# A graph layer with sorted edges: three searches for the node offsets instead of two, x split on GpSimd, eight edge blocks ahead of round 0

## The reference

```python
h = x @ W_node.T + b_node
e = edge_attr @ W_edge.T + b_edge
msg = (h[src] + e) @ W_msg.T + b_msg
s = segment_sum(msg, dst); deg = segment_sum(1, dst)
out = layernorm(x + s / maximum(deg, 1)[:, None])
```

## Time and profile before

| | before |
|---|---|
| median of 3 runs (lowest to highest) | 811.5 us (810.43 to 813.04) |
| profiled execution, time | 810.29 us |
| profiled execution, span | 808.4 us |
| busy: PE, weight load, DVE, ACT, POOL | 726.8, 643.4, 636.3, 461.0, 49.9 us |
| mean granted TensorE clock | 0.939 |
| moved by DMA | 121.08 MB |

### The profile page before, as it was taken

One profiled execution on the slowest core, in us unless ns is written; L12 is line 12 of the kernel. 1 busy time (PEld: TensorE's weight loads), 2 busy tenths in 40 slices (PEclk: granted clock), 3 DMA queues, 4 the chain that ended last, 5 costly groups with the idle time before them and its releaser, 6 DMA issues.

```text
span 808.4 us, 24794 instructions
## 1 busy us (share of the span) xinstructions
PE 726.8 (90%) x10555; PEld 643.4 (80%) x10555; DVE 636.3 (79%) x1128; ACT 461.0 (57%) x938; POOL 49.9 (6%) x42
## 2 busy tenths in 40 slices
PE   3454636999999999999999999999999999999995
PEld 2333435988898899889889888988888988898895
DVE  6564998798789878888888888878887887788732
ACT  4343632666566566565656665666666656565641
POOL 2002100000000000000000000000000000000000
PEclk9655657999999999999999999999999999999998
DMA  7987431544535444544553465346334544454300
GB/s 223 248 266 232 154 106 54 167 135 155 163 122 177 161 151 138 174 130 137 186 174 119 127 208 168 97 140 221 122 124 156 173 156 128 165 169 134 99 15 15
DMA packets 71529, 121.08 MB, mean 150 GB/s; under 512 B 4486, under 2 KB 17502, under 8 KB 71315
## 3 DMA queue, kind: packets, MB, share of 16 engines
q1 hardware_dynamic: 68462, 115.72, 44.8%
q0 software_dynamic: 2336, 2.83, 1.3%
q10 hardware_dynamic: 618, 0.90, 0.5%
HBM read 116.18 MB, written 3.23 MB: 148 GB/s over the span
## 4 chain that ended last, share of the span: by engine, by line
PE 85%; DVE 7%; DMA 4%; issue 2%; ACT 1%; ACTq 0%; DVEq 0%; POOLq 0%
PE x_ps L581 49%; PE count_ps L565 18%; PE win_ps L513 12%; PE win_ps L520 3%; DMA edges<-in_edge_attr_dram 2%; PE misc_ps L597 1%; PE misc_ps L598 1%; DVE key_hot L709 1%; DVE x_rest L879 1%; DMA win_src<-in_src_dram,clipped_int 1%; DVE row_hot L803 1%; DMA region<-in_dst_dram 1%; DVE row_hot L709 1%; DVE x_rest L873 1%; DMA starts_dram<-edge_total 1%
## 5 line engine op out<-in xcount | busy, mean ns | idle before, releaser
L1167 ACT CAST region<-count_ps 128x490 bf16<-128x490 f32 x625 | 350.2, 574 | 174.1 <-PE count_ps L565 168.0
L581 PE MATMUL x_ps<-region,x_rest 128*128 128x250 bf16 x2450 | 449.3, 270 | 0.0
L581 PE MATMUL x_ps<-region,x_hi 128*128 128x250 bf16 x1225 | 332.6, 271 | 0.0
L709 DVE TENSOR_TENSOR row_hot<-iota_bf,row 125x3200 bf16<-125x3200 bf16 x125 | 227.8, 1822 | 94.6 <-PE count_ps L565 64.3
L565 PE MATMUL count_ps<-key_hot,row_hot 125*128 125x98 bf16 x3125 | 244.2, 209 | 28.3 <-DVE key_hot L709 28.2
L565 PEld LDWEIGHTS count_ps<-key_hot,row_hot 125*128 125x128 bf16 x3125 | 199.8, 99 | 57.0 <-DVE key_hot L709 29.9
L581 PEld LDWEIGHTS x_ps<-region,x_rest 128*128 128x128 bf16 x2450 | 229.6, 98 | 17.4
L709 DVE TENSOR_TENSOR key_hot<-iota_bf,key 125x2500 bf16<-125x2500 bf16 x125 | 181.7, 1454 | 0.0
L513 PE MATMUL win_ps<-edges,onehot 128*32 128x128 f32 x3232 | 118.7, 292 | 11.2 <-DMA edges<-in_edge_attr_dram 9.4
L581 PEld LDWEIGHTS x_ps<-region,x_hi 128*128 128x128 bf16 x1225 | 118.9, 97 | 8.0
L513 PEld LDWEIGHTS win_ps<-edges,onehot 128*32 128x32 f32 x3232 | 89.0, 116 | 32.6 <-issue 21.8
(11 more groups left out here) (166 smaller groups left out, 318.6 us busy)
## 6 DMA issues: line engine op xcount, KB each, us to landing
edges<-in_edge_attr_dram SPq DMA_DIRECT2D x101, 1024.0 KB, 5.6
resid<-in_x_dram SPq DMA_DIRECT2D x25, 125.0 KB
out_dram<-y SPq DMA_DIRECT2D x25, 125.0 KB
region<-in_dst_dram ACTq DMA_DIRECT2D x1, 768.0 KB
win_src<-in_src_dram,clipped_int POOLq DMA_INDIRECT x25, 6.6
region<-in_L_gnn_W_node_dram SPq DMA_DIRECT2D x1, 64.0 KB
region<-in_L_gnn_W_edge_dram SPq DMA_DIRECT2D x1, 64.0 KB
region<-in_L_gnn_W_msg_dram SPq DMA_DIRECT2D x1, 64.0 KB
```

Source lines behind the costliest of these rows:

```text
L581: mm = pe.matmul(x_ps[m % 2][:, 0:NB], rows, counts[m % 2][:, b, :], start=(n == 0), stop=(n == PARTS - 1))
L709: ins = dve.tensor_tensor(hot[0:WE, g % 2, :, :].rearrange("p w (a b) -> p w a b", b=4), iota_bf[0:WE, 0:width].rearrange("p (c a b) -> p ...
L1167: act.copy(counts[m % 2][:, :, f * FILL * 2:(f + 1) * FILL * 2], count_ps[fill % COUNT_BANKS][:, 0:FILL * KEYS].rearrange("p (n b) -> p b ...
```

## The change

- `LEAD` is 8 instead of 11. The 93 other blocks lie in the 125 slots of the rounds, where 90 did; in rounds 0 and 1 there are four each, as before, in rounds 2 to 24 there are 85 instead of 82.
- Three searches: job 0 serves rounds 0 and 1 alone (5 columns, a window of 375 entries, columns of at most 332), job 1 rounds 2 to 17 (31 columns, 1375 entries, 13 columns on DVE and 18 on ACT), job 2 rounds 18 to 24 (14 columns, 750 entries, columns of at most 326). Job 0 is counted at block 1, job 1 in segments 0 to 2, job 2 in segments 4 and 5. All three windows are asked for in the lead; DVE prepares the block counts of job 1 (one instruction) ahead of the placing offsets of the first block.
- `x` (3.2 MB) is loaded behind block 3 instead of block 9, the weights behind block 6 instead of block 2; the weights are folded in segments 0 to 2 instead of blocks 4 to 6, and waited for at the first `apply_counts`.
- `split_rest` and `split_low` run on POOL, ahead of `load_window` of rounds 2 to 24. Their input, `copy_hi`, runs on ACT at blocks 5 to 7 and in segments 0 and 1. The first `apply_counts` still waits for all of them.
- `make_slots` of job 1 is in segment 5, of job 2 in segment 8, with the degrees, which wait for the latter; `make_keys(2)` moves from the second to the third segment of round 1.
- The checks move to segments 12 to 18; `check_order` reads the turned offsets (128x404, 4 parts) instead of the untouched ones (101x2048).
- Buffers: the windows lie elsewhere in `region`, `before_hot`, the junk outputs and `rows_words` have room of their own, and the turned slots and degrees go to `misc_ps` (`free_misc` is what PE waits for ahead of it).

```diff
-LEAD = 11
+LEAD = 8
-    JOB_K = (36, 14)
-    JOB_L = (1650, 825)
-    JOB_DVE = (18, 7)
+    JOB_K = (5, 31, 14)
+    JOB_L = (375, 1375, 750)
+    JOB_DVE = (3, 13, 4)
+    JOB_ROWS = (2, B_ROUNDS - 2, G0)
+    JOB_ROUND = (0, 2, B_ROUNDS)
+    SLOTS_B, SLOTS_A, DEGREES = 5, 8, 8
...
@@ sync
                 load_edges(t)
-                if t == 2:
+                if t == 3:
+                    load_x()
+                if t == 6:
                     load_small()
-                if t == 9:
-                    load_x()
...
@@ gpsimd
-            load_job(0)
-            load_job(1)
-            for m in range(ROUNDS):
+            def split_rest(i):
+                words = x_rest[:, i * 7:(i + 1) * 7, :].rearrange("p b d -> p (b d)")
+                pool.wait_ge(x_hi_ready, i + 1)
+                pool.tensor_tensor(words, words, x_hi[:, i * 7:(i + 1) * 7, :].rearrange("p b d -> p (b d)"), ALU.subtract).then_inc(x_rest_ready, 1)
+
+            def split_low(i):
+                words = x_rest[:, i * 7:(i + 1) * 7, :].rearrange("p b d -> p (b d)")
+                pool.wait_ge(x_rest_ready, i + 1)
+                lower, upper = halves(words)
+                pool.tensor_tensor(lower, words, upper, ALU.subtract).then_inc(x_ready, 1)
+
+            for k in range(JOBS):
+                load_job(k)
+            for m in range(2):
+                load_window(m)
+            for i in range(7):
+                split_rest(i)
+            for i in range(7):
+                split_low(i)
+            for m in range(2, ROUNDS):
                 load_window(m)
...
@@ tensor
+            def free_misc():
+                if ends[0] > 0:
+                    pe.wait_ge(msg_added, 2 * ends[0])
+                if turns[0] > 0:
+                    pe.wait_ge(keys_spread, turns[0])
+                if misc_slots[0] > 0:
+                    pe.wait_ge(src_index_ready, misc_slots[0])
+                if misc_degrees[0] > 0:
+                    pe.wait_ge(deg_copied, 1)
...
-                    if t == 8:
+                    if t == 4:
                         turn_slots(0)
                     place_windows(t)
-                    if t == 5:
-                        make_weights()
-                    if t == 9:
+                    if t == 6:
                         turn_keys(0)
...
+                    if f == 4 and g == 0:
+                        turn_weights()
+                    if f == 4 and g == 1:
+                        make_weights()
-                    if f == 3 and g == 2:
+                    if f == 1 and g == SLOTS_B:
+                        turn_slots(1)
+                    if f == 1 and g == SLOTS_A:
+                        turn_slots(2)
+                    if f == 3 and g == DEGREES:
                         turn_degrees()
-                        turn_slots(1)
...
@@ vector
             begin_job(0)
+            block_counts(1)
...
+                    if g < 3:
+                        count_nodes(1, [0, 4, 9][g], [4, 9, 13][g])
                     if g == 0:
+                        dve.wait_ge(wm_turned, 1)
+                        link(dve.tensor_copy(wm_t, x_ps[0][:, 0:D]))
...
+                    if g == 2:
+                        end_job(1)
+                        copy_weights()
+                        dve.sem_inc(early_done, 1)
+                    if g == 4:
+                        count_nodes(2, 0, JOB_DVE[2])
+                    if g == 5:
+                        make_slots(1)
+                        end_job(2)
+                    if g == SLOTS_A:
+                        make_slots(2)
                         make_degrees()
-                        check_order()
-                    if g == 1:
-                        check_sorted()
-                    if g == 2:
-                        make_slots(1)
-                        check_slots()
-                        copy_degrees()
-                        for i in range(7):
-                            split_rest(i)
-                    if g == 3:
-                        for i in range(7):
-                            split_low(i)
-                        dve.sem_inc(early_done, 1)
+                        copy_degrees()
...
@@ scalar
+                    if t == 1:
+                        sign_counts(0, JOB_DVE[0], JOB_K[0])
+                    if t == 2:
                         send_starts(0)
+                    if t == 3:
                         fetch_starts(0)
+                    if t >= 5:
+                        copy_hi(t - 5)
+                    if t == 6:
                         spread_keys(0)
...
-                if g in (1, 2):
-                    for i in range(4 * (g - 1), min(4 * g, 7)):
+                if g < 2:
+                    for i in range(3 + 2 * g, 5 + 2 * g):
                         copy_hi(i)
+                if g < 3:
+                    sign_counts(1, [13, 19, 25][g], [19, 25, 31][g])
+                if g == 3:
+                    send_starts(1)
+                if g == 4:
+                    fetch_starts(1)
+                    sign_counts(2, JOB_DVE[2], 9)
+                if g == 5:
+                    sign_counts(2, 9, JOB_K[2])
```

More of the change, by code:

```diff
@@ L146, in gnn_layer @@
         pos = sb("pos", [P, NS])
[L148 to L151, removed]
+        before_hot = [words.rearrange("p (j n) -> p j n", j=TILES) for words in before_words]
+        act_junk = [sb(f"act_junk{k}", [PB, 580], BF16) for k in range(2)]
+        dve_junk = [sb(f"dve_junk{k}", [PB, 580], BF16) for k in range(2)]
         is_last = sb("is_last", [P, 1])
@@ L166, in gnn_layer @@
[L166 to L171, removed]
+        lent = sb("lent", [P, 4 * P])
+        before_node = [lent[:, k * P:k * P + PB] for k in range(JOBS)]
@@ new lines, in gnn_layer @@
+        pos_nat = lent[:, 3 * P:4 * P].rearrange("p (q w) -> p q w", q=Q)
+        job_node = [sb(f"job_node{k}", [PB, JOB_K[k]]) for k in range(JOBS)]
+        job_half = [sb(f"job_half{k}", [PB, JOB_K[k]]) for k in range(JOBS)]
+        job_low = [sb(f"job_low{k}", [PB, JOB_K[k]]) for k in range(JOBS)]
+        job_high = [sb(f"job_high{k}", [PB, JOB_K[k]]) for k in range(JOBS)]
+        job_off = [sb(f"job_off{k}", [PB, JOB_K[k]]) for k in range(JOBS)]
+        job_cnt = [sb(f"job_cnt{k}", [PB, JOB_K[k]]) for k in range(JOBS)]
@@ L178, in gnn_layer @@
+        limit = [sb(f"limit{k}", [JOB_ROWS[k], 1]) for k in range(JOBS)]
         first_slot = sb("first_slot", [PB, 3, ROUNDS])
@@ L353, in halves, with window @@
             return both[:, :, 0], both[:, :, 1]
+        def window(k, i):
+            return max(0, LOWEST[k][0] * i + LOWEST[k][1]), HIGHEST[k][0] * i + HIGHEST[k][1]
         block = ctx.enter_context(nc.Block())
@@ L458, in load_window @@
             def load_window(m):
-                pool.wait_ge(src_index_ready, 1 if m < B_ROUNDS else 2)
+                pool.wait_ge(src_index_ready, 1 + sum(1 for r in JOB_ROUND[1:] if m >= r))
                 if m >= 3:
@@ new lines, in check_order @@
+            def check_order(i):
+                part = rel_col[:, 4 * i:4 * (i + 1), :]
+                junk = win_a.bitcast(BF16)[:, 0:4 * NS].rearrange("p (t c) -> p t c", t=4)
+                link(dve.tensor_scalar(junk, part, 0.0, None, ALU.is_ge))
+                link(dve.scalar_tensor_tensor(junk, part, float(W), junk, ALU.is_lt, ALU.mult, accum_out=inside[:, i:i + 1]))
+                if i == 3:
+                    link(dve.tensor_reduce(viol[:, 0:1], inside[:, :], AX.X, ALU.add))
```

292 lines of the change are left out of this document (145 added, 147 removed).

## The result

The changed kernel took 808.9 us (median of 10 runs, 805.22 to 810.03) beside 812.08 us for the kernel before (10 runs, 810.39 to 816.43): ratio 0.9946 (95% interval 0.9923 to 0.9969). The forecast was 796.8, range 788 to 807. The sign was right; of the forecast gain of some 15 us, 3 came. The profiled execution took 809.33 us, span 807.5, against the span of 808.4 before. The two profiled executions thus differ by 1 us only, the medians by 3.2: the one of before lay 1.8 us under its median of these ten runs, the one of after 0.4 above.

The account below looks back on a forecast made before the run. Data bounds the lead, DVE round 0, PE the rest. Lead -19.4, round 0 -8.6, POOL's pieces +4.9, round 1 +4, blocks +4.4 sum to -14.7: 795.6 profiled, 796.8 us median, range 788 to 807.

Parts of the forecast that it names:

- The sign: Whole kernel: faster, at a chance of 0.95; slower 0.04, within 0.3% 0.01.
- The lead: Stretch before round 0, bound by data: first hots at 61.8 instead of 81.2 us, -19.4 us.
- 12 us at 246 GB/s (2.95 MB), the other 3.41 MB at 295 GB/s: In the lead from 20.9 us: 6.36 MB moved at these rates, so block 4 has landed at 44.5 us.
- the rival with x holding up the slots: In the lead: x ahead of block 4 delays the slots more, at 6 us more 802.5 us; chance 0.1.
- The rate of 246: In the lead: the DMA rate in GB/s while windows of `dst` are fetched beside the edges, taken for 12 us.
- From block 4 to the first hots: End of the lead: slots turned, neighbour lists fetched and keys made between block 4's landing and first hots, 17.3 us.
- Round 0: First hots to first product with x: 38.4 us instead of 47.0 (-8.6), with POOL and DVE taking turns 43.3 (+4.9).
- Round 1: After the first product with x: new waits in segments 5 and 8 cost +4 us, from 0 to 7.
- The waits: Round 1, PE: for job 1's slots in segment 5, for job 2's slots and the degrees in segment 8, about 2 us.
- ACT's last columns: Round 1: DVE's `end_job(2)` waits for ACT's last five columns, about 1.5 us.
- Blocks: Rounds 2 to 24: three more blocks where PE is the limit, sums and placing, +4.4 us.
- A piece: One subtraction of x's split on POOL: 1.74 us, between bounds of 0.87 and 2.6.

Follow-up runs that it names:

- e5: The changed kernel with the windows of jobs 1 and 2 asked for only when x is in: 808.64 us (one run).
- e1: The changed kernel with x loaded behind block 7 and copied on ACT in segments 1 and 2 of round 0: 804.83 us.
- b1: The kernel before with only the 14 pieces of x's split moved to POOL, behind the windows of rounds 0 to 2: 817.09 us, ratio 1.0045.
- e6: The changed kernel with the edits of e1 and e4 together: 801.6 us, ratio 0.9873 to the kernel before.
- e9: e6 with each subtraction on POOL cut in two, 28 instead of 14: 802.33 us, ratio 0.9876 to the kernel before.
- e7: e1 with copies of x in segments 0 and 1 and job 2's window asked for behind the lists of rounds 0 and 1: 806.11 us.
- e2: The changed kernel without the 14 subtractions that split x; PE multiplies the upper part three times instead: 798.7 us (one run).
- e3: The changed kernel with the 14 subtractions back on DVE, in segments 2 and 3 of round 0: 815.33 us, ratio 1.0037 to the kernel before.
- e4: The changed kernel with the degrees turned in segment 9 and job 2's slots in segment 11, instead of both in segment 8: 804.56 us.

## Why the prediction was wrong

- **The lead: the step that failed is "12 us at 246 GB/s (2.95 MB), the other 3.41 MB at 295 GB/s".** It let the windows be done after 12 us and cost no more than in the kernel before. They took 23.0 and 20.3 us to land, and from 32 to 44 us all queues together moved 165 to 179 GB/s. Block 4 was summed at 52.85 instead of 44.5, 8.4 us of the 9.6 missing; e5, with the windows behind x, gives 42.03, e1, with x behind block 7, gives 44.04. So the delay needs both: the 3.2 MB of x ahead of block 4, and the low rate that comes with the windows. This was the rival with x holding up the slots (0.1, at 6 us, 802.5), and at 8 us it was worse than written.
- **The rate of 246 was one reading, and a high one.** The same stretch of b1, whose lead is that of the kernel before, moved 221 GB/s; from 32 to 40 us, with windows beside edge blocks and no x, e1 moved 184, e6 218, e9 230, and e7, with one window in flight, 243, and with x beside them the changed kernel moved 177, e2 181, e3 184 and e4 188. Why windows cost so much, at a full share of the engines, is open.
- **The rest of the lead.** From block 4 to the first hots I had 17.3 us. Without pieces it took 15.4 (e2) and 14.1 (e3), for one thing because the lists landed in 5.1 us and not in 7.1; with pieces it took 18.6. I counted POOL's pieces in round 0 alone, though three start in the lead; they stretch three instructions on its path.
- **Round 0: right in its sum, 43.63 against 43.3.** Uncontended 38.46 in e2. But what decided was another engine: POOL's last piece ended at 106.3, the product started at 115.07 behind DVE's hots. I added DVE's time to POOL's list, where the pieces stretch DVE's own list, with short instructions among the held, not only those with two inputs. That the sums agree within 0.3 us is in part luck.
- **Round 1: +7.6 for +4.** The waits came where they were named, 2.7 us, and some of DVE's (4.0 us for ACT's last columns, 1.5 forecast), with no idle PE beside it. Two terms were missing: the half speed behind the waits, 2.8 us, and PE's own work in the turns of the slots and degrees (0.81 + 0.51 + 0.41 = 1.7 us), which lay in round 0 before. Together that is 7.2 of the 7.6.
- **Blocks: +4.8 for +4.4,** confirmed.
- **A piece** took 1.87 and 2.11 us for 1.74; the estimate of 1.97 from the Trainium skill's page (GPSIMD Engine Reference, 3.1 Elementwise) was nearer. It moved nothing, since POOL didn't decide.

## What to carry to other kernels

A rate read in one stretch of one profile is no rate for another mix of transfers: read it in several runs, take the worst row as a bound, work out how long the slow transfer stays in flight, and ask which queue entry is issued late because of it. Work moved to GpSimd is not free on DVE: count the DVE instructions that fall beside it, the short ones above all, and place it beside those that are not held. A wait on a full PE can cost twice its length, if the clock falls behind it (here 2.7 us of waits and 2.8 of half speed); so put waits where their data has long arrived. When you cut an engine's work finer to spare another, look which of the two decides afterwards.

## What the hardware showed

- Windows of `dst` by an indirect DMA beside the 3.2 MB load of x: 165 to 179 GB/s from 32 to 44 us, at a share of 0.80 to 1.09, against 290 to 305 for x without them (e5, 28 to 40 us). Beside edge blocks and without x: 181 to 187 in e1, 246 and 221 in the lead of the kernel before and of b1. The offsets' way to DRAM and back lies in some of these stretches.
- DVE beside a GpSimd subtraction of 128x896: instructions of 0.22 to 0.35 us took 1.67 to 1.93, casts and compares with one tensor input too; a compare with an accumulator took its own 0.80.
- Cutting GpSimd's pieces in two raised their sum from 29.3 to 37.8 us, and lowered what one held DVE instruction lost from 1.5 us to about 0.75 (`key_hot` took 2.93 beside pieces, 2.18 beside halves, 1.45 alone).
